# Latent cross attention: key-weight products of two head groups together in the second and fourth batch of a tile, and layer-norm statistics one batch later

## The reference, cut to what matters

```python
x = x + xattn(layernorm(x), ctx)     # x: 64 x 32 x 512, ctx: 64 x 257 x 256
x = x + attn(layernorm(x))
x = x + ffn(layernorm(x))            # 8 experts, top 2

def xattn(x, z):                     # 16 heads of 32
    Q = x @ Wq.T
    K, V = z @ Wkv.T                 # Wkv: 1024 x 256
    A = softmax(Q K.T * 32 ** -0.5)  # per batch and head: 32 x 257
    return (A @ V) @ Wo.T
```

## Time and profile before

| | before |
|---|---|
| median of 3 runs | 1555.41 us |
| the profiled execution: its own time | 1554.73 us |
| its span, first to last instruction | 1553.0 us |
| mean granted TensorE clock over the span | 0.976 |
| PE busy | 1458.6 us (94%) |
| DVE busy | 1069.2 us (69%) |
| ACT busy | 827.5 us (53%) |
| POOL busy | 544.2 us (35%) |

### The profile page before, as it was taken

The page is one execution under the profiler, slowest core; times in us unless marked ns, Lnnn a source line. Parts: engine busy times, 40 slices in busy tenths (PEclk is TensorE's granted clock), DMA queues, the critical chain, the costliest instruction groups (busy, mean ns, idle before and its releaser), DMA issues. The chain is left out here.

```text
span 1553.0 us, 39528 instructions
## 1 busy us (share of the span) xinstructions
PE 1458.6 (94%) x14912; PEld 1295.2 (83%) x14912; DVE 1069.2 (69%) x1920; ACT 827.5 (53%) x1542; POOL 544.2 (35%) x816
## 2 busy tenths in 40 slices
PE   5899999999999999997899998679999999999997
PEld 4788888888888888885687876569999999999996
DVE  2566667666666666674567676687878878787884
ACT  3566666667666666663434342254554555555552
POOL 1122222222222222222866876443333332333232
PEclk8899999999999999998999999789999999999999
DMA  7101000100001010100011114147887778787871
GB/s 281 60 28 29 29 21 27 27 21 27 27 27 27 21 27 27 29 9 0 16 37 37 37 37 151 57 151 260 278 275 259 270 238 292 251 271 246 291 243 41
DMA packets 130734, 174.10 MB, mean 112 GB/s; under 512 B 16954, under 2 KB 89338, under 8 KB 130627
## 3 DMA queue, kind: packets, MB, share of 16 engines
q1 hardware_dynamic: 120242, 145.56, 28.8%
q0 software_dynamic: 10384, 27.05, 4.8%
HBM read 157.18 MB, written 19.06 MB: 113 GB/s over the span
## 5 line engine op out<-in xcount | busy, mean ns | idle before, releaser
L2037 DVE TENSOR_TENSOR lo<-raw,hi 128x1024 fp32r<-128x1024 f32 x207 | 246.1, 1220 | 7.0 <-ACT hi L1973 5.5
L52 PE MATMUL mo_bank<-xT_hi,hi 128*128 128x256 f32 x768 | 216.2, 282 | 3.5 <-DVE xT_lo L2046 2.8
L54 PE MATMUL mo_bank<-xT_lo,hi 128*128 128x256 f32 x768 | 215.1, 280 | 0.0
L53 PE MATMUL mo_bank<-xT_hi,lo 128*128 128x256 f32 x768 | 214.8, 280 | 0.0
L1973 ACT CAST hi<-raw 128x1024 fp32r<-128x1024 f32 x207 | 208.3, 1048 | 6.8 <-DMA raw<-in_L_ffn_W_dram 4.7
L565 ACT ACTIVATE Pr<-xa_s,nmax 128x257 f32<-128x257 f32 x256 | 119.1, 473 | 137.7 <-DVE nmax L655 137.6
L1993 ACT ACTIVATE sl<-mo_bank 128x256 f32<-128x256 f32 x117 | 45.1, 386 | 244.5 <-PE mo_bank L54 232.0
L52 PE MATMUL xa_s<-zT_hi,QK_hi 128*128 128x258 f32 x512 | 153.6, 300 | 8.8 <-DVE PT_lo L607 6.2
L52 PEld LDWEIGHTS mo_bank<-xT_hi,hi 128*128 128x128 f32 x768 | 144.7, 188 | 10.5 <-issue 5.9
L53 PEld LDWEIGHTS mo_bank<-xT_hi,lo 128*128 128x128 f32 x768 | 144.7, 188 | 3.3
L54 PEld LDWEIGHTS mo_bank<-xT_lo,hi 128*128 128x128 f32 x768 | 144.8, 189 | 0.0
(11 more groups left out here) (302 smaller groups left out, 3939.0 us busy)
## 6 DMA issues: line engine op xcount, KB each, us to landing
raw<-in_L_ffn_W_dram SPq DMA_DIRECT2D x207, 512.0 KB
raw<-in_ctx_dram SPq DMA_DIRECT2D x64, 256.0 KB, 2.6
out_dram<-x_res SPq DMA_DIRECT2D x16, 256.0 KB
xs<-xn SPq DMA_DIRECT2D x16, 256.0 KB
x_res<-in_x_dram SPq DMA_DIRECT2D x1, 3840.0 KB, 19.2
VL<-v_last_rows SPq DMA_DIRECT2D x128, 2.0 KB, 1.5
raw_o<-in_L_xattn_Wo_dram SPq DMA_DIRECT2D x1, 1024.0 KB, 5.8
raw_q<-in_L_xattn_Wq_dram SPq DMA_DIRECT2D x1, 1024.0 KB, 8.9
```

Source lines behind the costliest of these rows:

```text
L52: pe.matmul(out, lh, rh, start=start, stop=False)
L53: pe.matmul(out, ll, rh, start=False, stop=False)
L54: return pe.matmul(out, lh, rl, start=False, stop=stop)
L2037: vW.done(dve.tensor_tensor(lo, raw, hi.bitcast(F32), ALU.subtract), f"p{c}{q}")
```

## The change

Group pairs: absorptions are done two at a time, groups 2 and 3 of the next tile in the second batch and groups 0 and 1 of the tile after that in the fourth; the first and third batch have none. The second of a pair is written beside the first, in the other half of each of the four banks. The copies of a pair both wait for the second product. `AHEAD` goes from 5 to 6 (one more absorption before the first batch). On ACT, `z_hi` now stands before the copies and `u_out` behind them, in the second to fourth batch; in the first, `u_out` stays where it was, ahead of `qk_hi`. On DVE and POOL `statistics` and its `pow` go from the first batch to the second and `normalise` from the second to the third.

```diff
-        AHEAD = 5
+        AHEAD = 6
...
         def step_of(i, u, j, more):
-            if j < BT - 1:
-                return (1 - u, j + 1, 2 * (i + 1) + (j + 1) // 2 + 1) if more or u == 0 else None
-            return (u, 0, 2 * (i + 2) + 1) if more else None
+            if j == 1 and (more or u == 0):
+                return 1 - u, 2, 2 * (i + 1) + 2, BT * i + AHEAD + 2
+            if j == 3 and more:
+                return u, 0, 2 * (i + 2) + 1, BT * i + AHEAD + 4
+            return None
...
                 def absorb_k(q, m):
+                    at = (m % 2) * KL * P
...
-                            mm = pe.matmul(bank_s[:, hh, k * P:(k + 1) * P], Wk[r, m, k * P:(k + 1) * P],
+                            mm = pe.matmul(bank_s[:, hh, at + k * P:at + (k + 1) * P], Wk[r, m, k * P:(k + 1) * P],
...
                 for m in range(NQ):
-                    need(pe, a_QK, m)
+                    need(pe, a_QK, m - m % 2)
                     absorb_k(Qp[0], m)
...
                 absorb_k(Qp[1], 0)
+                absorb_k(Qp[1], 1)
                 pe.wait_ge(a_QK, AHEAD)
...
                         if step is not None:
-                            slot, m, q_count = step
+                            slot, m, q_count, _done = step
                             pe.wait_ge(a_E, 4 * s + 4)
                             pe.wait_ge(a_Q, q_count)
                             absorb_k(Qp[slot], m)
+                            absorb_k(Qp[slot], m + 1)
...
                         if step is not None:
-                            pe.wait_ge(a_QK, s + AHEAD + 1)
+                            pe.wait_ge(a_QK, step[3])
                         turn_p(s)
...
                 def qk_out(n, slot, m):
-                    act.wait_ge(pe_QK, n + 1)
+                    act.wait_ge(pe_QK, n - m % 2 + 2)
                     act.copy(QK[slot][:, :, 4 * m:4 * m + 4, :].rearrange("p k h t -> p h k t"),
-                             bank_s[:, :, 0:KL * P].rearrange("p h (k t) -> p h k t", k=KL)).then_inc(a_QK, 1)
+                             bank_s[:, :, (m % 2) * KL * P:(m % 2 + 1) * KL * P].rearrange("p h (k t) -> p h k t", k=KL)
+                             ).then_inc(a_QK, 1)
...
+                        if not (last and j == BT - 1):
+                            z_hi(s + 1)
+                        if step is not None:
+                            act.wait_ge(v_QK, s + 1)
+                            for n in range(2):
+                                qk_out(step[3] - 2 + n, step[0], step[1] + n)
                         if j > 0:
                             u_out(s - 1, j - 1)
-                        if step is not None:
-                            act.wait_ge(v_QK, s + 1)
-                            qk_out(s + AHEAD, step[0], step[1])
-                        if not (last and j == BT - 1):
-                            z_hi(s + 1)
...
-                        if j == 1 and more:
+                        if j == 2 and more:
                             normalise(dve, i + 2)
...
-                        if j == 0 and more:
+                        if j == 1 and more:
                             statistics(dve, i + 2)
...
-                        if j == 0 and more:
+                        if j == 1 and more:
                             rstd_of(pool, i + 2)
```

More of the change, by code:

```diff
@@ L553, in _ @@
                 qk_out(NQ, 1, 0)
+                qk_out(NQ + 1, 1, 1)
                 def tile(i, u, first, last, more):
```

## The result

The changed kernel takes 1551.22 us, the median of 7 runs (1549.42 to 1552.98), against 1555.22 us for the kernel before in 7 runs. The ratio is 0.9973, with a 95% interval from 0.9961 to 0.9984: a gain of 4.0 us, where a loss of 4.8 us was forecast. A second series, 12 runs against 28, gave 0.9982 (0.9971 to 0.9993).

A forecast was written before the change was run, and what follows sets the result against it. PE, busy 94% at full clock, was taken to bound the kernel. Thirteen full tiles +4.0, tile 14 -0.8, tile 0 +1.5 and set-up 0 sum to +4.8 us: 1559.5 us from 1554.73, range 1554.0 to 1564.0.

The forecast's parts named there:

- the size of the second absorption: Second and fourth batch on PE: the second absorption of each pair adds 0.65 us.
- the sum 0.65 + 0.85 up to the first copy: Fourth batch: second absorption 0.65 us, then 0.85 us from its start to the first copy's start on ACT.
- the set-up: Before the first scores: gains and an extra absorption and copy taken as 0, bounds -1.5 and +1.5 us.
- fourth +0.98: Fourth batch of a full tile: second absorption 0.65 us, turn_p's wait for both copies 0.29 us, restart 0.04 us.
- Tile 0: First tile: +1.5 us in all, chiefly +1.15 in the second batch, where nothing behind the pair covers the copies.
- signs of being wrong: Cross attention: fourth batch 10.3 us or less, full tile under 41.6 us, or a half-clock stretch beyond tile 0.
- The stall: Second batch: PE's wait for pt_lo, 0.63 us plus 0.1 for restarting, disappears without a successor.
- what tile 15 had shown: First batch of tile 15, without absorption or statistics: 10.09 us, taken as the new first-batch length against 10.38.
- Tile 14: Tile 14, costed apart: first batch -0.3, second +0.65, third -1.15, together -0.8 us.
- Copies covered: Fourth batch: both copies finish by project_q's end, batch +0.65, full tile -0.05, total 1554.5 us; chance 0.18.
- Every wait covered: Third batch's project_q does not wait for x_out either: full tile -0.37 us, total 1549.9 us; chance 0.07.
- Clock lost at the start: Tile 0: longer waits bring one or two half-clock stretches, 1.7 or 3.4 us, total 1561 to 1563 us; chance 0.09.

The follow-up runs named there:

- experiment 2: Kernel before with only the statistics, pow and normalise moved one batch later, single absorptions kept: 1548.93 us, ratio 0.9949.
- experiment 9: Changed kernel with PE's three remaining waits covered by reordering in the first, third and fourth batch: 1541.89 us, ratio 0.9901.
- one part gave 0.51%: Kernel before with only the statistics, pow and normalise moved one batch later: 1548.93 us, ratio 0.9949.
- the other took 0.33% back: Changed kernel with statistics, pow and normalise back in their old batches, pairs and new ACT order kept: 1562.11 us, ratio 1.0033.
- experiment 5: Changed kernel with the second batch's pair of absorptions done twice, four in a row, same values written: 1591.49 us in one run.
- experiment 10: Changed kernel with the second batch's pair of absorptions repeated only in every second tile: 1558.51 us in one run.
- experiment 4: Changed kernel with turn_z placed between the two absorptions of a pair instead of ahead of them: 1565.04 us, ratio 1.0049.
- experiments 7: Changed kernel with gather_z cut in halves and turn_x of the third batch put between them: 1546.19 us, ratio 0.9935.
- experiments 8: Kernel before with the statistics' move, single absorptions, and turn_x between the halves of gather_z in the third batch: 1545.04 us, ratio 0.9932.

## Why the prediction was wrong

**The failed step is the size of the second absorption.** It was put at 0.65 us "in any case", read from one absorption between full-array work. It costs 0.45 us. That enters twice a tile: as +0.65 in the second batch and, in the fourth, in the sum 0.65 + 0.85 up to the first copy, 1.50 us, for which the chip shows 539.92 - 538.68 = 1.24 us. With 0.45 in place of 0.65 the sum for a full tile would have been 0.31 - 2 x 0.20 = -0.09 us: this step alone turned the sign.

The trace of before could only give a bound: every absorption in the steady tiles stood alone. But one line in the waits of PE's weight loads had a hint, on average 0.18 us of idle in front of each of 60 absorptions with nothing that released it. In the changed kernel the same idle comes once in a pair, 31 times. First the kernel before, then the changed one:

```profile
PEld xa_s L377 <- issue: 10.9, 60, 1.0
...
PEld xa_s L381 <- issue: 6.0, 31, 1.0
```

What was missing is a lower bound on this term; all the bounds given were on the copies, the restarts and the set-up.

Batch by batch, forecast and measured change: first -0.29 and -0.31; second -0.08 and -0.25; third -0.33 and -0.37; fourth +0.98 and +0.70. A tile: +0.28 and -0.24 (with the 0.03 us for a restart, +0.31). Over 13 tiles this is 7.1 of the 8.8 us between forecast (+4.8) and result (-4.0). The second absorption's size is 13 x 0.40 = 5.2 of these; the rest are errors of 0.02 to 0.08 us a batch.

**A second term was mis-sized, and luck hid it.** Tile 0 was put at +1.5 us and took +4.2: by batch +1.24, +1.09, +1.09 and +0.76, where -0.3, +1.15, -0.3 and +1.0 stood in the sum. The set-up was put at 0 and took -1.9. Together they are +2.3, near the forecast's +1.5, by errors that cancel. What tile 0 lost beyond its forecast is the clock. PE waits 2.04 us for the copy before the first scores (before: 1.12) and 2.10 us for the pair's copies in the second batch (before: 1.19), and the scores behind each of the two waits took 4.50 and 4.47 us in place of 3.0. Busy time by stretch in these two scores of the changed kernel, granted clock third from the end; in the kernel before it is 1.00 in both:

```profile
45.70:50.10 4.40, 4.40 (x24) 4.40 (x25) 0.69 (x1) 1.02 (x4) 0.00 (x0) 0.61 0.00 0
66.50:70.90 4.40, 4.40 (x27) 4.40 (x25) 1.98 (x3) 2.01 (x7) 0.00 (x0) 0.61 0.23 63
```

**What held.** Of the prediction's own signs of being wrong one came: a full tile under 41.6 us; the fourth batch, at 10.37, stayed above 10.3. The stall went and had no successor (experiment 2: 0.73 us, forecast 0.73). The first batch took what tile 15 had shown. The third batch gained half of its absorption and waited for `x_out` for the rest (`project_q` starts 529.70 - 528.42 = 1.28 us after `turn_x`, forecast 1.30 from the earlier trace rows). `turn_p` waits for the copies in the fourth batch: `project_q` to `turn_p` is 541.90 - 539.78 = 2.12 us in place of 1.88. Its 0.24 us are near the 0.29 forecast because two errors cancel: the copies came 0.25 us sooner (3.22 us after the pair's start, not 3.47), and PE had 0.20 us less to do. Tile 14: -1.05, forecast -0.8.

**The rivals.** Copies covered: no, the wait is there. Every wait covered: its 1549.9 us lies nearest to the result, but by number alone; all the waits came, and experiment 9 shows what it takes to cover them. Clock lost at the start: this happened, two stretches of 1.5 us where the rival had priced one at 1.7 and two at 3.4, and the set-up hid it. From 45 to 88 us the mean granted clock is 0.88, before it was 0.96 from 48 to 86 us. In the steady tiles it held full speed, with three short waits in each, as the busy time by stretch of the changed kernel shows (us, PE, PEld, DVE, ACT, POOL, then the granted clock):

```profile
88.00:625.00 537.00, 530.40 (x4836) 471.01 (x4835) 361.20 (x637) 356.30 (x781) 128.64 (x273) 1.00 0.09 26
```

The Trainium skill ("TensorE: Matmul & The Clock Gate", on the second failure mode) tells of a kernel in which frequent short idles between groups of matmuls made the clock swing. The trace doesn't bear that out here: three waits of 0.2 to 0.3 us a tile left the granted clock at 1.00 over 537 us.

## What to carry to other kernels

The cost of a small operation, read between two neighbours of another shape, contains the change to and fro; doing two of them back to back costs less than twice, and removing one can win more than its own rows say (here 0.85 for a recorded 0.65 between full-array products). When a change has two parts, cost and try them apart: here one part gave 0.51% and the other took 0.33% back. Batching an operation whose result others wait for paid here only with the order changed as well, so that each new wait had other work in front of it. And check the terms of a sum one by one even where their total fits: start-up was near its forecast here by two errors of 1.9 and 2.7 us.

## What the runs showed of the hardware

**With a longer loop body PE waited at the loop's turn.** With 32 more absorption matmuls in the source for each turn of the loop over two tiles (experiment 5; 809 recorded matmuls a turn against 747 and as many weight loads, the 32-row ones being recorded as two each), the scores after the fourth batch of tiles 3, 5, 7, 9 and 11 came late. Timeline of PE, the first product of tile 8:

```profile
393.17 0.55 PE L52 MATMUL xa_s<-zT_hi,QK_hi 128*128 128x258 f32 x1 [2.85 <-issue]
```

There is no releaser. The same in PE's waits over the span:

```profile
PE xa_s L52 <- issue: 15.1, 5, 3.2
```

With half as many extra instructions (experiment 10, 779 matmuls a turn) it is not there at all, so it is not in proportion to the length. Each of the two is a single run. The page of each profile points at the fetching of instructions: its DMA queue of the kind "instruction" moved 75 packets in experiment 10, 74 in every other kernel here, and 120 in experiment 5 (packets, MB, share). The changed kernel, then experiment 5:

```profile
q8 instruction: 74, 1.21, 0.3%
...
q8 instruction: 120, 1.97, 0.5%
```

That these transfers are what PE waits for was not tried, and why the turns behind tiles 1 and 13 have no wait is open. Four of the five waits cost the clock too, in a stage where it otherwise never falls; busy time by stretch, granted clock third from the end:

```profile
389.00:393.00 4.00, 1.25 (x10) 0.86 (x8) 1.95 (x6) 2.35 (x5) 0.49 (x1) 0.95 0.21 70
393.00:396.00 3.00, 2.83 (x13) 2.87 (x14) 0.00 (x0) 0.00 (x0) 0.00 (x0) 0.50 0.02 5
```

After a wait of 2.85 us PE worked at the half level, 1.2 GHz. After the wait of 2.73 us ahead of tile 4 it did not: the granted clock of those scores is 1.00 and the batch took 10.08 us. The first batches of tiles 6, 8, 10 and 12 took 11.32, 11.31, 12.67 and 11.55 us in place of 10.07, together 6.6 us more. Tiles 1 to 13 took 571.75 us in place of 537.22: of the 34.5 us the products explain 13 x 0.89 = 11.6, the five waits 16.4 by PE's starts, and these four batches the rest.

**The change of shape.** Going from full-array matmuls to absorptions on 32 rows and back costs about 0.4 us (0.35 in experiment 4, 0.41 from experiments 7 and 8), of which the rows of the absorption itself show half. Ahead of `values`, whose products are themselves on part of the array (128*32), a lone absorption cost 0.62 us all in (experiments 8 and 9, with orders changed as well), so the price depends on the neighbours. What in the engine takes that time stays open.
